# The last steps of a routed vision block: new order of choices and ranks, weight splitting inside the tiles, and pads from two queues

## The reference

```python
# x (64, 2, 104, 104); B = 64 images, 169 tokens each, D = 128
h = tokens(x)                 # image, 4 shifted copies, normalised over the image, * gamma + beta,
                              # 8x8 convolution with stride 8 -> (64, 169, 128)
h = h + attention(layernorm(h))   # 8 heads, linear: q', k' = exp(q proj), exp(k proj);
                              # out = q' (k'^T v) / (q' sum k' + 1e-6), then Wout and bias
def ffn(x, Wg, W, V, W2):     # E = 8 experts, D = 128, F = 512, two experts a token
    topv, topi = top_k(x @ Wg, 2)
    w = softmax(topv)
    for e in range(8):
        y += gw[..., e:e+1] * ((silu(x @ W[e]) * (x @ V[e])) @ W2[e])
h = h + ffn(layernorm(h))
```

## Time and profile before

| | us |
|---|---|
| median of 3 runs | 1215.3 (1210.65 to 1218.12) |
| profiled execution | 1215.14 |
| its span, first to last instruction | 1213.4 |
| PE busy | 1116.5 (92%) |
| DVE busy | 834.5 (69%) |
| ACT busy | 567.8 (47%) |
| POOL busy | 605.7 (50%) |

### The profile page before, as it was taken

The page is one execution under the profiler, slowest core; times in us unless marked ns, Lnnn a source line. Parts: engine busy times, 40 slices in busy tenths (PEclk is TensorE's granted clock), DMA queues, the critical chain, the costliest instruction groups (busy, mean ns, idle before and its releaser), DMA issues.

```text
span 1213.4 us, 30866 instructions
## 1 busy us (share of the span) xinstructions
PE 1116.5 (92%) x9016; PEld 966.7 (80%) x9017; DVE 834.5 (69%) x3198; ACT 567.8 (47%) x1318; POOL 605.7 (50%) x666
## 2 busy tenths in 40 slices
PE   2699999999999999999999834999999999999994
PEld 1567777777777777777777634999999999999994
DVE  4447777777777777777766574777777777777773
ACT  2343534435435344354333423555555555555552
POOL 2001535353535353535353552666766666666664
PEclk9799999999999999999999966999999999999997
DMA  9251131130301311201010134444443444434442
GB/s 156 54 158 40 33 72 32 42 64 26 79 26 34 72 33 43 62 26 34 26 33 26 38 87 92 54 54 53 56 54 52 55 53 56 54 52 54 55 54 22
DMA packets 75795, 65.86 MB, mean 54 GB/s; under 512 B 12382, under 2 KB 66718, under 8 KB 75712
## 3 DMA queue, kind: packets, MB, share of 16 engines
q0 software_dynamic: 33024, 25.86, 15.2%
q1 hardware_dynamic: 42496, 38.59, 13.9%
q10 hardware_dynamic: 192, 0.37, 0.2%
HBM read 33.07 MB, written 31.71 MB: 53 GB/s over the span
## 4 chain that ended last, share of the span: by engine, by line
PE 86%; DVE 3%; issue 2%; SPq 1%; DMA 1%; ACT 1%; POOL 0%; POOLq 0%; DVEq 0%; ACTq 0%
PE bank L1243 21%; PE bank L1255 13%; PE bank L539 8%; PE bank L585 6%; PE bank L644 5%; PE bank L631 4%; PE bank L657 4%; PE bank L501 4%; PE bank L632 4%; PE bank L633 4%; PE bank L650 3%; DVE patches L748 2%; PE bank L425 2%; PE bank L532 2%; PE bank L1231 2%
## 5 line engine op out<-in xcount | busy, mean ns | idle before, releaser
L1384 POOL DMA_INDIRECT out_rows<-yo,dest x184 | 302.9, 1646 | 169.1 <-issue 116.4
L1243 PE MATMUL bank<-xT_e,wv 128*128 128x256 f32 x2208 | 289.9, 287 | 0.9 <-DVE xT_e L1335 0.9
L1243 PEld LDWEIGHTS bank<-xT_e,wv 128*128 128x128 f32 x2208 | 272.5, 190 | 1.4 <-DVE xT_e L1335 1.3
L1147 POOL DMA_INDIRECT sorted_rows<-xrow_all,sloti x192 | 188.8, 983 | 73.2 <-issue 54.8
L1313 ACT ACTIVATE sil<-bank 128x256 f32<-128x256 f32 x368 | 141.5, 384 | 160.5 <-PE bank L1243 156.7
L1342 DVE TENSOR_TENSOR hid<-sil,bank 128x256 f32<-128x256 f32 x368 | 154.8, 421 | 84.6 <-ACT sil L1313 74.2
L1255 PE MATMUL bank<-w,hid 128*128 x1472 | 179.5, 275 | 1.0 <-DVE hid L1342 1.0
L1120 POOL TENSOR_SCALAR vare<-mv 128x3 f32<-128x3 f32 x64 | 12.5, 195 | 324.1 <-issue 267.9
L1255 PEld LDWEIGHTS bank<-w,hid 128*128 128x128 f32 x1472 | 171.6, 192 | 1.2 <-issue 1.2
L1298 ACT CAST wv<-wv_all 128x1024 fp32r x92 | 96.5, 1049 | 41.0 <-issue 28.0
L1058 ACT ACTIVATE attn<-bank 128x256 f32<-128x256 f32 x128 | 49.4, 386 | 130.8 <-PE bank L633 130.8
(11 more groups left out here) (187 smaller groups left out, 1835.7 us busy)
## 6 DMA issues: line engine op xcount, KB each, us to landing
xr<-sorted_rows SPq DMA_DIRECT2D x92, 130.0 KB
raw<-in_x SPq DMA_DIRECT2D x64, 84.5 KB
raw<-in_x SPq DMA_DIRECT2D x60, 78.0 KB
out_rows<-attn SPq DMA_DIRECT2D x64, 58.5 KB
sorted_rows<-xrow_all,sloti POOLq DMA_INDIRECT x192, 2.4
out_rows<-yo,dest POOLq DMA_INDIRECT x184
wv_all<-in_L_ffn_W SPq DMA_DIRECT2D x8, 256.0 KB, 5.1
wv_all<-in_L_ffn_V SPq DMA_DIRECT2D x8, 256.0 KB, 5.2
```

What stands on the lines that cost most here:

```text
L1147: po.indirect_dma_start(sorted_rows, bass.IndirectOffsetOnAxis(sloti[:, p, j, ch:ch + 1], 0), xrow[:, p, j, ch], None).then_inc(s(f"scatte ...
L1243: q = pe.matmul(bank[fc][:, TT * m:TT * m + TT], wv[:, p, w_, m, cols], xT[:, p, x_], start=(w_ + x_ == 0), stop=(w_ == 1))
L1384: po.indirect_dma_start(out, bass.IndirectOffsetOnAxis(dest[:, p, a:a + 1], 0), yo[:, p, a], None, compute_op=ALU.add).then_inc(s(f"added{ ...
```

## The change

In steps 32 to 34 the pieces of weight splitting (`lo_high`, `lo_low`, `wl_all`) go. DVE's order there changes: `choose` comes to the front of steps 33 and 34, and in step 32 behind the denominators and the normal rows; the normal rows come behind the denominators. PE's rank matmuls come ahead of the broadcasts (33, 34) or behind the keys (32). POOL scatters three chunks ahead of its root in step 32 and two in step 33, instead of one. The down weights are issued at the start of SP's step 32. The pads are issued half by SP and half by ACT; ACT first does one small Silu. SP reads the first two row numbers before it waits for pads and scatters. In the tiles `high_w` comes ahead of the four Silus, and `low_w` subtracts out of `wv_all`.

```diff
+        def pad_ends(eng, of_experts):
+            for e in of_experts:
+                r = eng.value_load(ends[0:1, e:e + 1], min_val=e * CAP, max_val=e * CAP + NTOK)
+                eng.dma_start(sorted_rows[bass.ds(r, TT)].rearrange("(a p) n -> p a n", a=2), pad).then_inc(s("pads_out"), 16)
...
+                if n == NPAIR:
+                    sp.wait_ge(s("conv_done"), NPAIR)
+                    for e in range(E):
+                        expert_sync(sp, "down_weights", e)
...
-            sp.wait_ge(s("conv_done"), NPAIR)
-            for e in range(E):
-                expert_sync(sp, "down_weights", e)
-
             sp.wait_ge(s("ends_ready"), 1)
-            for e in range(E):
-                r = sp.value_load(ends[0:1, e:e + 1], min_val=e * CAP, max_val=e * CAP + NTOK)
-                sp.dma_start(sorted_rows[bass.ds(r, TT)].rearrange("(a p) n -> p a n", a=2), pad).then_inc(s("pads_out"), 16)
+            pad_ends(sp, range(0, E, 2))
             for q in range(2):
                 sp.wait_ge(s(f"h2_out{q}"), NPAIR // 2 * 16 * len(PLACES))
+            sp.wait_ge(s("table_ready"), 2)
+            first = [expert_sync(sp, "row_number", t) for t in range(2)]
             sp.wait_ge(s("pads_out"), 16 * (1 + E))
             for q in range(2):
                 sp.wait_ge(s(f"scattered{q}"), NPAIR // 2 * 96)
-            sp.wait_ge(s("table_ready"), 2)
-            expert_sync(sp, "rows", 0)
+            expert_sync(sp, "rows", first)
...
+                if d and not a and not b:
+                    rank()
                 if c:
                     pe.wait_ge(s("rden_ready"), mc + 1)
                     broadcast(0)
...
+                if b and d and not a:
+                    rank()
...
-                    if d and i == 1:
...
+                if a and d and i == 1:
+                    rank()
...
-                if not a:
-                    lo_low(ve, n - NPAIR, 0)
-                if d:
+                def normal_rows():
                     ve.wait_ge(s("ln2_rstd"), md + 1)
...
+                if d and a:
+                    normal_rows()
+                if n > NPAIR:
+                    choose(md)
                 if c:
                     ve.wait_ge(s("d8_done"), mc + 1)
...
+                if d and not a:
+                    normal_rows()
+                if n == NPAIR:
+                    choose(md)
...
-                if d:
+                if d and a:
                     choose(md)
...
+            ac.wait_ge(s("egap_ready"), NPAIR)
+            ac.activation(esum_silu[:], egap[:], ACT.Silu)
+            ac.wait_ge(s("ends_ready"), 1)
+            pad_ends(ac, range(1, E, 2))
             expert_scalar(ac)
...
+                before_root = {NPAIR: 3, NPAIR + 1: 2}.get(n, 1)
-                    scatter((0,))
+                    scatter(range(before_root))
...
-                    scatter((1, 2))
+                    scatter(range(before_root, NCH))
...
         def step(t, h, p, more, prev):
+            if more:
+                high_w(t + 1, 1 - p)
             for fc in range(4):
                 if more and fc == 2:
                     copy_x(t + 1, h + p, 1 - p)
-                    high_w(t + 1, 1 - p)
                 ac.wait_ge(s("hv_done"), 4 * t + fc + 1)
...
         def low_w(t, p):
             e = expert_of(ve, t)
+            ve.wait_ge(s("w_high"), t + 1)
             at_least(ve, s("hv_done"), 4 * (t - 1))
-            ve.tensor_copy(wv[:, p, 1].rearrange("p m n -> p (m n)"),
-                           wl_all[:, bass.ds(e, 1)].rearrange("p e m n -> p (e m n)")).then_inc(s("w_low"), 1)
+            ve.tensor_tensor(wv[:, p, 1].rearrange("p m n -> p (m n)"),
+                             wv_all[:, bass.ds(e, 1)].rearrange("p e m n -> p (e m n)"),
+                             wv[:, p, 0].rearrange("p m n -> p (m n)").bitcast(F32), ALU.subtract).then_inc(s("w_low"), 1)
```

More of the change, by code:

```diff
@@ L360, in _ @@
             sp.wait_ge(s("const_in"), 16)
-            pad = K("padrow").rearrange("p (a n) -> p a n", a=2)
             sp.dma_start(sorted_rows[E * CAP:E * CAP + TT].rearrange("(a p) n -> p a n", a=2), pad).then_inc(s("pads_out"), 16)
@@ L511, in q_feature, with rank @@
                              lambda a_: xT[:, pb, a_, 0:QW]).then_inc(s("q_mm"), 1)
+                def rank():
+                    pe.wait_ge(s("before_step"), NCH * (md + 1))
+                    if a:
+                        pe.wait_ge(s("ln1_x"), n + 1)
+                    else:
+                        pe.wait_ge(s("h2_copied"), n - 2)
+                        pe.wait_ge(s("logit_read"), n - 2)
+                    pe.matmul(ranks[:, :], ones, before[:].rearrange("p c e -> p (c e)"), start=True, stop=False)
+                    pe.matmul(ranks[:, 0:NCH * E], tri, both[:].rearrange("p c e -> p (c e)"), start=False, stop=True
+                              ).then_inc(s("rank_done"), 1)
                 if n == 1:
@@ L588, in step @@
                             t.then_inc(s("out_done"), 1)
-                    if d and i == 1:
-                        pe.wait_ge(s("before_step"), NCH * (md + 1))
-                        if a:
-                            pe.wait_ge(s("ln1_x"), n + 1)
-                        else:
-                            pe.wait_ge(s("h2_copied"), n - 2)
-                            pe.wait_ge(s("logit_read"), n - 2)
-                        pe.matmul(ranks[:, :], ones, before[:].rearrange("p c e -> p (c e)"), start=True, stop=False)
-                        pe.matmul(ranks[:, 0:NCH * E], tri, both[:].rearrange("p c e -> p (c e)"), start=False, stop=True
-                                  ).then_inc(s("rank_done"), 1)
+                    if a and d and i == 1:
+                        rank()
                 if b:
@@ L839, in step @@
                     normalise(1)
-                if not a:
-                    lo_low(ve, n - NPAIR, 1)
                 front(0)
@@ L862, in step @@
                                      ).then_inc(s("xT_low"), 1)
-                if not a:
-                    lo_low(ve, n - NPAIR, 2)
                 if d:
@@ L1060, in q_exponent @@
                                   ACT.Exp).then_inc(s("q_exp"), 1)
-                if not a:
-                    lo_high(ac, n - NPAIR, 0)
                 if b:
@@ L1077, in step @@
                     image_norm(g + 1, 1)
-                if not a:
-                    lo_high(ac, n - NPAIR, 1)
                 if d:
@@ L1093, in step @@
                     image_norm(g + 1, 0)
-                if not a:
-                    lo_high(ac, n - NPAIR, 2)
                 if b:
@@ L1211, in sync, with row_number, rows @@
             return
-        def rows(t, h, p):
-            r = sp.value_load(table[0:1, bass.ds(t, 1), 0], min_val=0, max_val=E * CAP)
+        def row_number(t):
+            return sp.value_load(table[0:1, bass.ds(t, 1), 0], min_val=0, max_val=E * CAP)
+        if what == "row_number":
+            return row_number(e)
+        def rows(t, h, p, r=None):
+            if r is None:
+                r = row_number(t)
             at_least(sp, s("tok_t"), t - 1)
@@ L1218, in rows @@
                          ).then_inc(s(f"rows_in{p}"), 16)
-        rows(0, 0, 0)
-        rows(1, 0, 1)
+        rows(0, 0, 0, e[0])
+        rows(1, 0, 1, e[1])
         with sp.Fori(0, (NT - 2) // 2) as i:
@@ L1272, in tensor @@
         down(NT - 1, 1, expert_of(pe, NT - 1))
-    PLACES_LOW = {(0, 1): (0, 2), (0, 2): (2, 4), (1, 0): (4, 6), (1, 1): (6, 8), (1, 2): (8, 10),
-                  (2, 0): (10, 12), (2, 1): (12, 14), (2, 2): (14, 16)}
-    def lo_high(ac, n, place):
-        for k in range(*PLACES_LOW.get((n, place), (0, 0))):
-            if k == 0:
-                ac.wait_ge(s("conv_done"), NPAIR)
-                ac.wait_ge(s("weights_in"), 16 * 2 * E)
-            at_least(ac, s("lo_split"), k - 7)
-            ac.copy(wv[:, k // 4 % 2, k // 2 % 2, k % 2], wv_all[:, k // 2, k % 2]).then_inc(s("lo_rounded"), 1)
-    def lo_low(ve, n, place):
-        for k in range(*PLACES_LOW.get((n, place), (0, 0))):
-            ve.wait_ge(s("lo_rounded"), k + 1)
-            if k == 0:
-                ve.wait_ge(s("weights_in"), 16 * 2 * E)
-            ve.tensor_tensor(wl_all[:, k // 2, k % 2], wv_all[:, k // 2, k % 2],
-                             wv[:, k // 4 % 2, k // 2 % 2, k % 2].bitcast(F32), ALU.subtract).then_inc(s("lo_split"), 1)
     def scalar(ac):
```

12 lines of the change are left out of this document (7 added, 5 removed).

## The result

| | before | after |
|---|---|---|
| median of 4 runs, us | 1213.9 (1210.65 to 1218.12) | 1243.2 (1240.66 to 1244.6) |
| profiled execution, its span | 1215.1, 1213.4 | 1243.1, 1240.7 |
| start of the last convolution to the first turn of rows on PE | 84.05 | 74.64 |
| first turn to the end of the span | 469.9 | 508.4 |
| PE busy, ACT busy | 1116.5, 567.8 | 1126.2, 545.8 |

What follows compares the result with a forecast made beforehand. PE bounds the token loop and expert phase; the seam between them, where PE idles, ends in a DMA chain. Profiled 1215.1 - 13 (seam) + 15.7 (tiles) + 1.1 (scaling) = 1218.9, say 1219 us; range 1203 to 1230.

Steps and rivals of the forecast that it cites:

- the tiles: Expert phase after the seam: subtracting low weights in each tile costs 0.18 us a tile, 87 x 0.18 = 15.7 us.
- The seam: Token-loop steps 32 to 34 and the start of the tiles, where PE idles: 13 us won, range 10 to 15.
- the high weights are issued behind Silu 3, at 0.69: On ACT in each tile: rounding starts 0.69 us after Silu 3's start (0.38 Silu, 0.31 register load).
- d: Lateness of PE's first matmul of the next tile, paid once per two tiles: 0.30 to 0.44 us.
- the scaling: Output scaling right behind the low weights in the tiles comes 1.1 us later, counted once.
- 87 to 88 waits: PE at the hidden products in the tiles: waits for DVE's low weights of 0.3 to 0.4 us each.
- Rival B: Tiles hold 4.88 us because register load or DVE instructions overlap more; 1203 us, from 1200 to 1206; chance 0.24.
- Rival C: Tiles: subtraction at its upper bound 1.37 and full refill, d 0.59 and more, 0.3 a tile; 1229 us; chance 0.18.
- the low clock: PE's clock down in step 33, L585 taking 4.87 us: slots and ends 8.0 us earlier, seam gain 12.3.
- the scatter's landing: End of the seam: last scatter lands 3.35 us from issue, taken from the last tiles' accumulating write.
- upper loss: Seam: pads (1.06 MB) and scatters (0.4 MB) share engines, 10 us from 719, ending a microsecond after the scatters.
- Rival D: Seam: pads, scatters and output rows on three queues crowd the engines; only 6 us won, 1226 us; chance 0.05.

Runs made afterwards that it cites:

- the seam alone: Changed kernel, but the high weights are rounded at their old place and DVE copies 1024 elements instead of subtracting; 1203.4 us, ratio 0.992.

## Why the prediction was wrong, point by point

The forecast span was 1217.2, the measured one is 1240.7. Of the 23.5 us between them 21.7 lie in the tiles. The seam fell short by 3.6, and 1.8 of that came back by luck, from the earlier start of the last convolution.

**The tiles: mechanism right, the term mis-sized.** That the way through rounding and subtraction would end behind PE's need, at `hidden`, at clock 1.00 and at every second tile boundary of the chain, is what happened, and the subtraction's 1.22 us, a value interpolated from its 256 and 512 element forms, measured 1.225. The failing step is "the high weights are issued behind Silu 3, at 0.69", and the term that it mis-sized is d, with the price of a tile that hangs on it. I took the register load of the earlier trace rows (0.31) as all that stands in front of the rounding, because it was all that stood there before; but before, the rounding sat in the middle of the loop's body. At its head it gets the loop's edge in front of it, 0.39 us in every second tile, and 0.41 instead of 0.31 in the others. So the rounding of the first tile in the table began at 1.19 and not at 0.69. d became 0.86 instead of 0.36: a tile cost 0.43 and not 0.18, 87 x 0.43 = 37.4 and not 15.7. The chains that ended last show it directly: from the first turn to the last down products on them PE takes 440.6 us before (743.50 to 1184.11) and 478.9 after (732.25 to 1211.10), 38.2 more, about 44 pairs of tiles at 0.87. Behind that, POOL's adds run 29.3 and 29.6 us to the end. The 1.1 that I had added for the scaling is not there; 0.3 is.

The number of waits was wrong as well. I had worked out d per two tiles, and then expected 87 to 88 waits of 0.3 to 0.4 with tiles of 5.06; the measured 44 waits of 0.6 with tiles of 4.88 and 5.75 in turn are the form that the argument should have led to. The restart of PE took 0.25 where up to 0.1 was allowed for the weight load.

**Rival B** (tiles hold 4.88) is what none of the kernels with two buffers and the subtraction did and four buffers could. **Rival C** had the right sign and d of 0.59 and more, but its cause, a subtraction of 1.37, is refuted by 1.225. Its price per tile (0.3) was still too low. The range ended at 1230 because its upper cases changed only the duration of the subtraction; nothing in it widened the place on ACT where the chain begins.

**The seam: mechanism right, one term mis-sized, and luck in where it ended.** From the start of the last convolution to the ends of the experts' rows the gain is 7.8 us (66.01 to 58.19), forecast 8.0 for the low clock, and the low clock is what the trace shows (L607 at 4.68); at the attention sum of step 33 the gain is 4.4 (54.01 to 49.65), forecast 4.3. The last releaser is a scatter, as forecast. The first turn came at 732.25, inside 728.5 to 733.5, but with before's start of the last convolution it would have come at 734.1, outside. The failing term is the scatter's landing: 6.20 us from issue against 3.35. In the other kernels with this seam it took 4.17 to 5.55. In before, the last scatter was followed by 10.38 us to the first turn, now by 8.79; I had counted on 6.1; that is 2.7 of the 3.6 us. Another 0.7 is that I took 13 where the sum for the low clock was 12.3. That pads and scatters crowd the same engines had been put down as an upper loss only, and is what happened. From the last convolution to the first turn the gain is 9.4 in after and 11.4 in the seam alone, between them the run's own scatter; after lies below my range of 10 to 15. Rival D (only 6 won, by crowding) has its mechanism confirmed and its size not.

**What the parts are worth.** Up to the ends of the experts' rows the missing splits bring 5.9 us (66.01 to 60.14) and the new order 1.9 (60.14 to 58.19), of which none is left at the first turn in after. Behind them the down weights' early load brings 2.7 to 4.7 us, and the second queue for the pads between nothing and 1.3. No run had the splits back in the new kernel; their price rests on the kernel with the old order, against before. The parts of the seam were undone in one run each.

**Open.** Why the last scatter needs 6.20 us in after and 4.2 in the seam alone, with the same instructions in the seam, is not settled; nor is why a loop's edge costs ACT 0.39 us. And what step 33 would take at full clock was not reached by any kernel.

By the Trainium skill (VectorE: DVE Perf Modes, "The perf-mode tier table") a two-operand fp32 operation never runs at a copy's doubled rate. This case's runs agree: 1.225 us for the subtraction of 1024 elements against 0.69 for the copy of as many, and exchanging the one for the other moved the end by 24 us (508.4 to 484.4).

## What to carry to other kernels

In a software pipeline with two buffers, follow the way from the release of a buffer to its next use over all engines, with every wait of a buffer (here the two of `sil`) and with the edge of the loop where an instruction stands at its head; busy shares say nothing of it, since PE's busy share fell by 6% while no other engine was over 0.72. When an edit frees memory, spend it on distance: four buffers, with the work put further ahead, turned a loss of 2.4% into a gain of 0.6% with the same work per tile. And an instruction that is moved does not keep the idle time that stood before it in its old place.

## What the runs showed of the hardware

- The edge of a loop on ACT costs 0.39 us in front of the first instruction (0.80 against 0.41; here the first instruction is the rounding, with its register load), and the trace puts it down to the semaphore that the instruction names, though it had been up for long. It was seen by its period: every second tile, and every fourth with four in the body.
- The last scatter lands between 2.82 and 6.20 us after its issue. The shortest time is that with the pads nearly through (DMA share 0.34); between 4.17 and 6.20, with the same instructions under way, the runs differ without a reason that they show.
- An fp32 matmul call on 512 columns shows as two matmuls and takes 0.93 us at a granted clock of 1.00 (3.70 for four calls).
- A pause of 0.62 us on PE costs 0.25 more in the twelve matmuls behind it (1.69 against 1.44), and a pause of 0.08 costs the same 0.25.
